# Message stage of a two-layer graph kernel: one semaphore wait per iteration instead of four ahead of GpSimd's row gathers

## The reference

```
x = silu(edge_radial @ W1 + b1)          # per edge, 8 -> 64
x = silu(x @ W2 + b2)                    # 64 -> 64
tpw = x @ W3 + b3                        # 64 -> 256: four 8x8 matrices per edge
hs_e, hv_e = hs[src], hv[src]            # gathered rows of the source nodes
m0 = ALPHA * (einsum(hs_e * sh0, W00) + INV_SQRT3 * einsum(hv_e, sh1, W110))
m1 = ALPHA * (einsum(hs_e, sh1, W01) + einsum(hv_e * sh0, W10))
agg = segment_sum(concat(m0, m1), dst) / 4
h = layernorm(x + h_self + agg)
```

## Time and profile before

| | |
|---|---|
| median of 3 runs | 8416.13 us (8414.13 to 8420.86) |
| the profiled execution | 8425.42 us, span 8423.6 us, mean granted TensorE clock 0.888 |
| busy: PE, DVE, ACT, POOL | 80%, 77%, 33%, 64% of the span |
| chain that ended last | PE 59%, issue 16%, unknown queue 9%, DVE 8%, ACT 6%, POOL 1% |
| message stage, slices 1 to 23 of 40 | PE 6 to 7 tenths busy, DVE 7 to 8, POOL 5 to 6 |
| gathers of the message stage (L475, `early<-in_x_wide`) | 2870, 977 ns each |

### The profile page before, as it was taken

The page is one execution under the profiler, slowest core; times in us unless marked ns, Lnnn a source line. Parts: engine busy times, 40 slices in busy tenths (PEclk is TensorE's granted clock), DMA queues, the critical chain, the costliest instruction groups (busy, mean ns, idle before and its releaser), DMA issues.

```text
span 8423.6 us, 93644 instructions
## 1 busy us (share of the span) xinstructions
PE 6705.5 (80%) x26126; PEld 5191.3 (62%) x26126; DVE 6512.7 (77%) x11130; ACT 2820.1 (33%) x4982; POOL 5375.5 (64%) x5400
## 2 busy tenths in 40 slices
PE   6777777777777777777777508999999999999992
PEld 4555555555555555555555407888888888888881
DVE  7888877888878787888787537878787788787874
ACT  4555555555545545544444201111111111111110
POOL 5666666666656666666565566666666666666666
PEclk8888888888888888888888659999999999999996
DMA  2222122222222211211111202222222222222221
GB/s 62 42 41 42 40 41 42 42 42 41 41 39 42 41 41 38 42 39 35 34 33 32 48 18 47 50 51 48 48 53 48 48 48 53 48 48 53 48 48 27
DMA packets 318658, 363.23 MB, mean 43 GB/s; under 512 B 157447, under 2 KB 259511, under 8 KB 317963
## 3 DMA queue, kind: packets, MB, share of 16 engines
q0 software_dynamic: 175840, 136.07, 12.2%
q1 hardware_dynamic: 142794, 226.94, 8.4%
HBM read 251.38 MB, written 111.20 MB: 43 GB/s over the span
## 4 chain that ended last, share of the span: by engine, by line
PE 59%; issue 16%; another core or an unknown queue 9%; DVE 8%; ACT 6%; POOL 1%; DMA 1%; ACTq 0%; DVEq 0%; SPq 0%; POOLq 0%
PE tpw L662 26%; PE tpw L595 12%; PE hid L662 8%; PE hid L604 4%; PE hid L585 4%; PE hid L581 4%; ACT early L685 2%; ACT nearx L707 1%; POOL msgs L475 1%; ACT hid L679 1%; DVE early L974 1%; DVE prod L962 1%; DVE msgs L1023 1%; DVE prod L953 1%
## 5 line engine op out<-in xcount | busy, mean ns | idle before, releaser
L475 POOL DMA_INDIRECT early<-in_x_wide,idx x2870 | 2803.5, 977 | 1793.9 <-issue 1724.5
L475 POOL DMA_INDIRECT prod<-table,idx x2125 | 2180.5, 1026 | 1023.1 <-issue 597.1
L662 PE MATMUL tpw<-highs,hot 128*128 128x462 f32 x5250 | 1993.8, 380 | 78.1 <-issue 62.1
L662 PE MATMUL tpw<-lows,hot 128*128 128x462 f32 x5250 | 1979.3, 377 | 50.9 <-issue 50.3
L595 PE MATMUL tpw<-w3s,early 128*128 128x256 f32 x6252 | 1842.4, 455 | 6.9 <-issue 6.9
L595 PEld LDWEIGHTS tpw<-w3s,early 128*128 128x128 f32 x6252 | 1384.4, 229 | 575.5 <-issue 341.9
L662 PEld LDWEIGHTS tpw<-highs,hot 128*128 128x128 f32 x5250 | 1007.2, 192 | 234.7 <-issue 107.0
L662 PEld LDWEIGHTS tpw<-lows,hot 128*128 128x128 f32 x5250 | 1002.1, 191 | 186.1 <-issue 75.4
L685 ACT ACTIVATE early<-hid,b2s 64x384 f32<-64x384 f32 x1042 | 601.5, 577 | 1008.9 <-PE hid L585 570.1
L581 PE MATMUL hid<-early,w1s 16*128 16x384 f32 x1044 | 546.3, 607 | 485.3 <-ACT early L685 410.0
L585 PE MATMUL hid<-hid,w2s 128*128 128x384 f32 x1042 | 499.2, 563 | 500.2 <-ACT hid L679 274.0
(11 more groups left out here) (186 smaller groups left out, 8729.0 us busy)
## 6 DMA issues: line engine op xcount, KB each, us to landing
big<-qrows SPq DMA_DIRECT2D x126, 512.0 KB
scan<-prod SPq DMA_DIRECT2D x125, 425.0 KB
scan<-sums SPq DMA_DIRECT2D x130, 384.0 KB
early<-in_x_wide,idx POOLq DMA_INDIRECT x2870
prod<-table,idx POOLq DMA_INDIRECT x2125
qbx<-qx SPq DMA_DIRECT2D x131, 128.0 KB
early<-in_radial_t SPq DMA_DIRECT2D x262, 48.0 KB
sh<-in_sh SPq DMA_DIRECT2D x131, 48.0 KB
```

The costliest lines, as they stand in the source:

```text
L475: return pool.indirect_dma_start(out=dest, out_offset=None, in_=source, in_offset=bass.IndirectOffsetOnAxis(ap=index, axis=0))
L662: mm = pe.matmul(found[i][:, 0:BC], hot(c)[:, g, at:at + P], split(s, g), start=g == 0 and s == 0, stop=g == NBATCH - 1 and s == SPLITS - 1)
```

## The change

GpSimd's waits in `gather_again` are cut from two kinds to one: the wait for `tpw_ready` is kept at k = 0 alone, and neither k = 2 (`tpw_ready`) nor k = 1 and 3 (`layers_done`) has one any more. The wait for `tpw_used`, which protects the rows in use, stays at all four.

```
             def gather_again(it, k, m, loads, all_tiles=False):
                 pool.wait_ge(tpw_used, it * SLOTS + k - 1)
-                if k % HALF == 0:
-                    pool.wait_ge(tpw_ready, it * SLOTS + k - 1)
-                else:
-                    pool.wait_ge(layers_done, it * SLOTS + k)
+                if k == 0:
+                    pool.wait_ge(tpw_ready, it * SLOTS - 1)
                 if k == 0:
                     pool.wait_ge(idx_in[m], loads * 16 + 16)
                 pool.nop(nofuse=True)
                 gather_tiles(m, k, all_tiles)
```

## The result

The changed kernel takes 9804.91 us (median; 9777.22 to 9809.86) where the kernel before, measured beside it, takes 8415.13 us (8413.39 to 8420.86): a ratio of 1.1643 with the interval [1.1621, 1.1666], 1390 us more. The profiled execution took 9809.86 us. From L491 on its lines have numbers two lower than before (L679 is now L677, L685 L683, L935 L933).

The account below looks back on a forecast made before the run. Bound: TensorE, nearly stopped some 10 us into unbroken gathers, recovering about 2 us after. 99 x (14.86 - 1.6, second hold given back) + 28 x (13.61 - 1.6) = 1649 us onto 8425.4, less 9.3 to the median: 10,065; range 8600 to 10,650.

Parts of the forecast that it names:

- Waits at k = 1 and 3: GpSimd's message stage: removing these waits for `layers_done` saves two semaphore instructions and changes nothing, bounds 0 and 0.
- One run of 23 and one pause: GpSimd's message stage: gathers join into one run of 28.45 us, with one pause of some 20 us per iteration.
- The pause at k = 2 is what frees TensorE: GpSimd's message stage: the 2.81 us pause is no lost time, since it lets TensorE's held completions go.
- Release 1.96 us after the run: Message stage: TensorE's held results come 1.96 us after the run's last gather, so 30.41 us after its first.
- The bound above: Upper bound: recovery after a long run takes 6.05 us instead of 1.96, adding 520 us: 10,585.
- Full hold of 14.86 us in every iteration: Message stage: TensorE released 14.86 us later in 99 iterations with `dst_row`, 13.61 in 28 without; chance 0.68.
- rival 1: Trickle: TensorE passes instructions slowly during the long run, ScalarE goes on inside it; 8607 to 9500, chance 0.16.
- L679's late updates from 697.6 to some 2,400 us: Sign of being right: ScalarE's "remote" idle at L679 grows to some 2,400 us, starts about 2 us after the run.
- PE and DVE near 5 tenths, second layer unchanged: Sign of being right: TensorE and VectorE near 5 tenths busy in the message stage, the second layer's stage unchanged.
- Rivals 2 and 3: 2: hold has its own period or another wait stops GpSimd, 8416; 3: hold ends by itself, 8213; chance 0.08 each.
- rival 3: Message stage: hold ends by itself at 3031, only the quiet second half remains, 203 us less, 8213; chance 0.08.
- The instruction refill: TensorE's slow issue during 98 gathers could be its refill; by the mostly-hidden rule the change costs nothing, about 8416.

Follow-up runs that it names:

- the run of 17: Kernel before with only the wait at k = 2 removed, so GpSimd's longest run is 17 gathers: 9276.02 us, ratio 1.1017.

## Why the prediction was right, and where its sum was off

The sign, the place and the core of the mechanism held: GpSimd's pause is what frees TensorE. 10,065 us were forecast and 9804.91 measured, +1649 against +1390. That the hold lasts until the run ends did not hold, and one of the text's own signs of being wrong came true: L677 starts in mid-run in 48 of its 61 late starts.

- **Waits at k = 1 and 3, nothing.** Right: 1.0006 [0.9997, 1.0016].
- **One run of 23 and one pause.** Right: 28.55 us by the rows against 28.45. The pause was put at 20 us; it is near 22 in long iterations and 12 in short ones.
- **The pause at k = 2 is what frees TensorE.** Right, and shown: memsets in its place bring 1372 of 1390 us back (1390 less the 18 us left in another group).
- **Release 1.96 us after the run.** Off: where a result came only after 23 gathers, the second layer's came mostly 4.1 us after, between the 1.96 of eleven and the 6.05 of 98. The bound above had allowed for that.
- **Full hold of 14.86 us in every iteration.** This is the term that was mis-sized, and the step that the text itself called the weakest: that the hold grows in step with the run. It does in half of the iterations. The 66 long ones are near 51.3 us, 15.1 above the 36.17 of before, where full hold with a release at 4.1 us gives 14.86 + 2.14 - 1.6 = 15.4. The 63 short ones are near 41.5, only 5.3 above. 66 x 15.1 + 63 x 5.3 = 1331 us, the message stage's 1330. The fit of the long ones is partly luck: it leaves out that TensorE comes back at the lower clock (below), and in the iteration shown the first layer came out before the run ended. And two errors pull in opposite directions: the later release, 2.14 us more in each of these, made up for a part of what the short iterations fell short by. In the short ones the first layer escapes the hold and the second trickles out in mid-run: rival 1, at its lower end, in every second iteration. The forecast took full hold and trickle for alternatives; they were a mixture. Over all iterations the stage lost 10.47 us each, where the sum had 13.0 (1649 / 127).
- **L679's late updates from 697.6 to some 2,400 us, with starts about 2 us after the run.** Wrong as put: 1007.9 (L677), and most starts inside the run. The sum was right (2120 at L677 and L683 together); the sign had been tied to one line, while the hold catches whichever layer is due. It should have been stated for TensorE's consumers together.
- **PE and DVE near 5 tenths, second layer unchanged.** PE 5 to 6, DVE 6; 3308 us against 3303.
- **Rivals 2 and 3.** A hold with a period of its own is excluded by the memsets, and by the run of 17. Nothing of rival 3 was seen where TensorE is held. On the chip without holds the outcome is rival 2's number (0.9997), for a reason that no text had: the hold depends on the chip.
- **The instruction refill.** The prediction had set the rule of the Trainium skill's page "Runtime: NRT & Kernel Launch", section "Instruction fetch mechanics", against a hold, with 8416 us. The measurement decided against that number, but not against the rule that the refill is mostly hidden: 23 instruction packets in the whole execution are too few for a loss in every iteration, which is in keeping with it. So the refill isn't what makes this loss. In the stretch of the 88.21 us of the earlier trace rows two such packets do fall (4766 to 4896 us), and those rows alone don't tell whether the refill has a part there.

**Open:** which part of the chip makes TensorE's updates wait while GpSimd issues gathers, and whether the matmuls themselves are late or only their announcements; why chips differ; how short a pause suffices (0.95 us, six gathers into a run, wasn't enough to lift the hold; after eleven it couldn't be tried where holds exist); and why long and short iterations alternate. No version that computes the same beat both kernels: those with pauses are equal or slower.

## What to carry to other kernels

A wait that looks redundant by data can be the pause that another engine lives on: before removing one, look at what happens in the gap that it makes, and at the distance from the gap's start to the first result of every other engine. Where GpSimd issues many indirect gathers in a row, look for late updates of TensorE ("remote"); if there are any, break the gathers after about eleven by some 3 us of other work of GpSimd, or of waiting, and check that the rows still land in time. These are the sizes that worked in this kernel; others weren't mapped. And measure such a change on more than one chip: the same pair of kernels differed by 16% in one comparison and by nothing on another chip.

## What the runs showed of the hardware that was not expected

- An unbroken run of indirect gathers by GpSimd (1.25 us each) holds TensorE's semaphore updates back. Inside a long run results still pass, but late: the first layer issued at 3347.19 came through at 3364.39. The release is 1.8 to 2.3 us after a run of eleven or twelve in the rows shown, mostly 4.1 us after 23 for the second layer, 6.05 us after 98.
- Other work of GpSimd doesn't hold it (memsets, 3.10 us), and fewer bytes per gather don't lift it (192 or 4 per row: 9805 and 10,193 us).
- Not every chip does it. Three groups had the kernel before at 8415 to 8427 us, with holds; two groups on one other chip had it at 7908 us, with none in their kernels' traces.
- After a long hold TensorE works at the lower of its two clock levels (1.2 GHz): in the iteration shown it had issued nothing for 14.14 us before the second layer of 3365.03, and the granted clock is 0.50 from 3372.00 to 3378.50 us where it was 1.00 from 3346.00 to 3352.00. The twelve third-layer matmuls take 5.49 us at 3372.98 and 2.86 us at 3348.03, and the granted clock of the message stage fell from 0.87 to 0.79. The forecast's sum had no term for it; how much of the loss it makes wasn't measured.
